# The seam between an attention stage and the dense tiles after it, reordered: the first tile's products inside the last attention pair, router logits in halves, butterflies in eight pieces

## What is computed

```python
x = x + tanh(g_xattn[0]) * ssm(ctx, layernorm(x));   x = x + tanh(g_ffn[0]) * quantised_ffn(layernorm(x))
x = x + tanh(g_xattn[1]) * attention16heads(layernorm(x), ctx)
x = x + tanh(g_ffn[1])   * moe(layernorm(x))          # 16 experts, top 4, + shared expert
x = x + tanh(g_xattn[2]) * map2(layernorm(x));        x = x + tanh(g_ffn[2]) * (fwht(silu(x@W1.T) * (x@W3.T)) @ W2.T)
x = x + tanh(g_xattn[3]) * map3(layernorm(x));        x = x + tanh(g_ffn[3]) * moe2(layernorm(x))   # 8 experts, top 2

# moe: logits = x @ gate_w.T; p = softmax(logits); the top k of p, renormalised, weigh the experts
#      h = silu(x @ w_gate.T) * (x @ w_up.T);  y += (h @ w_down.T) * weight[token, expert]
```

## Time and profile before

| | |
|---|---|
| three executions | 1054.9, 1059.25, 1060.66 us, median 1059.25 |
| the profiled execution | 1060.62 us, span 1058.4 us, mean granted clock 0.945 |
| busy | PE 940.8 (89%), DVE 729.5 (69%), ACT 646.8 (61%), POOL 485.2 (46%) |
| attention, a steady pair | 8.5 us |
| dense tiles | from 540.3 us to the end |
| clock slices | PE clock at 9 or 8 tenths only at the start, at the seam and at 565 to 595 us |

### The profile page before, as it was taken

One profiled execution on the slowest core, in us unless ns is written; L12 is line 12 of the kernel. 1 busy time (PEld: TensorE's weight loads), 2 busy tenths in 40 slices (PEclk: granted clock), 3 DMA queues, 4 the chain that ended last, 5 costly groups with the idle time before them and its releaser, 6 DMA issues.

```text
span 1058.4 us, 15635 instructions
## 1 busy us (share of the span) xinstructions
PE 940.8 (89%) x5402; PEld 768.4 (73%) x5402; DVE 729.5 (69%) x1309; ACT 646.8 (61%) x1251; POOL 485.2 (46%) x480
## 2 busy tenths in 40 slices
PE   5376677568999999999889999899999999999997
PEld 1033233346999999999878888787788888888886
DVE  6799998885777777776565765774565565666644
ACT  5857664665777777777535666545557545544553
POOL 0266551143666666765343334453343444444442
PEclk8599989687999999999889999999999999999999
DMA  9200100004000000000036000000000410000000
GB/s 314 113 0 1 60 1 0 1 1 176 2 2 1 2 1 1 2 1 2 1 134 264 1 1 1 1 2 1 1 1 1 166 58 2 1 2 1 20 1 21
DMA packets 4562, 35.92 MB, mean 34 GB/s; under 512 B 1021, under 2 KB 2149, under 8 KB 3109
## 3 DMA queue, kind: packets, MB, share of 16 engines
q1 hardware_dynamic: 4485, 34.93, 8.5%
HBM read 33.88 MB, written 1.05 MB: 33 GB/s over the span
## 4 chain that ended last, share of the span: by engine, by line
PE 47%; DVE 17%; issue 8%; POOL 8%; ACT 4%; DVEq 0%; POOLq 0%; ACTq 0%
PE psum L387 13%; PE psum L388 13%; PE psum L389 13%; POOL a_P L1890 3%; DVE a_max L1614 2%; POOL a_rk L1823 2%; POOL a_rq L1831 2%; DVE psum L1739 2%; DVE f_silu L1757 2%; PE psum L691 1%; PE psum L766 1%; PE psum L783 1%; PE psum L639 1%; ACT L1191 1%; PE psum L730 1%
## 5 line engine op out<-in xcount | busy, mean ns | idle before, releaser
L387 PE MATMUL psum<-x_norm_T_hi,f_wgu_hi 128*128 128x512 f32 x400 | 173.5, 434 | 3.8 <-DVE f_h_lo L1746 3.5
L388 PE MATMUL psum<-x_norm_T_lo,f_wgu_hi 128*128 128x512 f32 x400 | 158.9, 397 | 0.0
L389 PE MATMUL psum<-x_norm_T_hi,f_wgu_lo 128*128 128x512 f32 x400 | 158.4, 396 | 0.0
L826 ACT ACTIVATE f_h_hi<-psum 128x512 fp32r<-128x512 f32 x100 | 59.5, 595 | 107.7 <-DVE psum L1739 107.6
L387 PE MATMUL psum<-f_wd_hi,f_h_hi 128*128 128x256 f32 x400 | 121.5, 304 | 1.1 <-DVE f_h_lo L1746 0.9
L1746 DVE TENSOR_TENSOR f_h_lo<-psum,f_h_hi 128x512 fp32r<-128x512 f32 x100 | 69.0, 690 | 63.5 <-ACT f_h_hi L826 63.4
L388 PE MATMUL psum<-f_wd_lo,f_h_hi 128*128 128x256 f32 x400 | 112.7, 282 | 0.0
L389 PE MATMUL psum<-f_wd_hi,f_h_lo 128*128 128x256 f32 x400 | 112.6, 281 | 0.0
L1912 POOL TENSOR_TENSOR m_dBu<-m_du,m_Bs 128x1024 f32<-128x1024 f32 x32 | 76.1, 2381 | 69.2 <-DVE m_du L1333 24.8
L1836 POOL TENSOR_TENSOR f_wgu_lo<-f_w,f_wgu_hi 128x512 fp32r<-128x512 f32 x44 | 56.7, 1288 | 97.4 <-ACT f_wgu_hi L826 97.4
L1836 POOL TENSOR_TENSOR f_wgu_lo<-f_wb,f_wgu_hi 128x512 fp32r<-128x512 f32 x36 | 46.6, 1293 | 116.1 <-ACT f_wgu_hi L826 116.1
(11 more groups left out here) (329 smaller groups left out, 2716.6 us busy)
## 6 DMA issues: line engine op xcount, KB each, us to landing
f_wb<-in_f1b SPq DMA_DIRECT2D x1, 6912.0 KB, 20.1
f_w<-in_f3w SPq DMA_DIRECT2D x1, 5376.0 KB, 17.8
f_wa<-in_f1a SPq DMA_DIRECT2D x1, 3840.0 KB, 14.2
w_raw<-in_w0raw SPq DMA_DIRECT2D x1, 3072.0 KB, 18.5
f_w<-in_f2w SPq DMA_DIRECT2D x1, 3072.0 KB, 25.3
a_wo<-in_wo SPq DMA_DIRECT2D x2, 1024.0 KB, 13.1
a_wq<-in_wq SPq DMA_DIRECT2D x1, 2048.0 KB, 26.4
x_res<-in_x SPq DMA_DIRECT2D x1, 1024.0 KB, 8.9
```

The source lines that it names most:

```text
L387: mm(out, wh, xh, start=start, stop=False, **kw)
L388: mm(out, wh, xl, start=False, stop=False, **kw)
L389: return mm(out, wl, xh, start=False, stop=stop, **kw)
L826: return A(out_, in_, ACT.Copy)
```

## The change

The order of work changes; the number of matmuls and their shapes don't. DVE gets 12 more instructions.

- At the seam, `gate_up(0)` and the transposes of the combine weights go ahead of the last probability transposes (step 32), `combine(0)` and `gate_up(1)` ahead of the last output product (step 33). The last AC goes to bank 6, `combine(0)` to bank 7. ACT and POOL make the parts of tile 0 earlier, ACT loads the silu table in step 32.
- Router logits are two halves of 12 matmuls at two places.
- On DVE, `take_logits` moves behind the query sums, `router_top` ahead of `a_AC_lo` of step 31, `router_split` ahead of the last reciprocal, the residual of half 1 behind tile 1's `f_silu*up`.
- Beside the tiles, `aT` and `apply` of layer 2, half 0, leave the places of map steps; a normalise moves by one place; the four butterflies of two column blocks become eight of one, five of them at tiles 28 to 37.

```diff
+    AC_BANK = [4] * (HEADS2 - 1) + [6]
@@ the places
-    put_norm(1, 1, 3, 5, 6, 7, 9, 10, 13, 15, 18)
+    put_norm(1, 1, 3, 5, 6, 7, 8, 9, 10, 13, 15, 18)
-    put_attention(2, 0, P1 + 2, P1 + 4, P1 + 8, P1 + 12, P1 + 16, P1 + 20, P1 + 24)
+    put_attention(2, 0, P1 + 2, P1 + 4, P1 + 8, P1 + 13, P1 + 15, P1 + 18, P1 + 22)
-    for n, p in enumerate((44, 48, 52, P1)):
+    for n, p in enumerate((44, 48, 52, P1, P1 + 6, P1 + 10, P1 + 14, P1 + 19)):
         put(p, "butterfly", n)
-    put_norm(2, 0, P1 + 30, P1 + 32, P1 + 35, P1 + 37)
+    put_norm(2, 0, P1 + 30, P1 + 33, P1 + 35, P1 + 37)
@@ PE, attn1
                 if i == KB + 2:
-                    router_logits(1, 0).then_inc(S("b7_put"), 1)
+                    router_logits(1, 0, 0)
...
+                if i == HEADS2 - 2:
+                    router_logits(1, 0, 2).then_inc(S("b7_put"), 1)
                 if i + 1 < HEADS2:
                     query_sums(i + 1)
+                if i == HEADS2:
+                    pe.wait_ge(S("a_exp"), HEADS2)
+                    gate_up(0)
+                    pe.wait_ge(S("a_kT"), HEADS2)
+                    pe.wait_ge(S("f_cmb"), 1)
+                    combine_T(cmb_of(1, 0)).then_inc(S("b7_put"), 1)
...
-                if i == HEADS2:
-                    combine_T(cmb_of(1, 0)).then_inc(S("b7_put"), 1)
-                if i == HEADS2 + 1:
-                    gate_up(0)
...
+                if i == HEADS2 + 1:
+                    combine(0)
+                    gate_up(1)
@@ ACT, attn1
+                if i == HEADS2 - 1:
+                    gu_hi(0)
+                if i == HEADS2:
+                    A(scratch[:, 20:21], epsc[:, :], ACT.Silu)
+                    gu_hi(1)
+                    silu(0)
@@ DVE, attn1
+                if i == HEADS2 - 1:
+                    router_top(1, 0)
                 if i >= 2:
                     ac_lo(i - 2)
...
-                    router_top(1, 0)
+                    router_split(1, 0)
                 dve.wait_ge(S("a_exp"), i + 1)
...
-            router_split(1, 0)
...
+            silu_up(0)
@@ DVE, ffns
-                if g == 0:
+                if g == 1:
                     dve.wait_ge(S("a_out"), HEADS2)
                     residual("A1", 1)
@@ POOL
+                    if i == HEADS2 - 1:
+                        gu_lo(0)
```

More of the change, by code:

```diff
@@ L578, in gate_up, with combine, router_logits @@
                 last.then_inc(S("f_up" if b else "f_gate"), 1)
-        def router_logits(l, h):
+        def combine(g):
+            l, h, q, j = FT[g]
+            if not WEIGHTED[g]:
+                return
+            if j == (0 if l == 1 else J3S):
+                pe.wait_ge(S("b7_free"), bank7.index(("cmbT", l, h)) + 1)
+                loaded(pe, f"sel{l}")
+            if ROUTED[g]:
+                pe.wait_ge(S("f_h"), ROUTED[g])
+            mm(ps[:, 6 if g else 7, :], sel[l][:, j, :], cmbT[h][:, :], start=True, stop=True).then_inc(S("f_cw"), 1)
+        def router_logits(l, h, t0):
             xh, xl = xTp[h]
             pe.wait_ge(S("r_w"), 1 if l == 1 else 2)
-            for t in range(TH):
+            for t in (t0, t0 + 1):
                 sl = slice(t * P, (t + 1) * P)
@@ L732, in side @@
                     _, l, h = w
-                    use_bank7(w)
-                    last = router_logits(l, h)
+                    last = router_logits(l, h, 2)
+                elif kind == "logits_half":
+                    _, l, h = w
+                    use_bank7(("logits", l, h))
+                    router_logits(l, h, 0)
+                    continue
                 elif kind == "cmbT":
@@ L772, in ffns @@
         def ffns(k):
[L773 to L783, removed]
             def down(g):
@@ L1046, in d_hi, with silu @@
             copy(wdh[g % 3][:, :], raw_w(l, j)[:, GU:WJ]).then_inc(S("f_wdh"), 1)
+        def silu(g):
+            act.wait_ge(S("f_gate"), g + 1)
+            if g >= 2:
+                act.wait_ge(S("f_h" if WEIGHTED[g - 2] else "f_m"), ROUTED[g - 2] + 1 if WEIGHTED[g - 2] else g - 1)
+            A(sg[g % 2][:, :], ps[:, 2 + 2 * (g % 2), :], ACT.Silu).then_inc(S("f_sg"), 1)
         def router_exp(l, h):
@@ L1186, in ffns @@
                     rows_hi(g - 1)
-                if g < FN:
-                    act.wait_ge(S("f_gate"), g + 1)
-                    if g >= 2:
-                        act.wait_ge(S("f_h" if WEIGHTED[g - 2] else "f_m"), ROUTED[g - 2] + 1 if WEIGHTED[g - 2] else g - 1)
-                    A(sg[g % 2][:, :], ps[:, 2 + 2 * (g % 2), :], ACT.Silu).then_inc(S("f_sg"), 1)
+                if 0 < g < FN:
+                    silu(g)
                 side(2 * g)
@@ L1540, in router_split, with silu_up @@
             V.tensor_tensor(cmb[:, :, 64:64 + n], rr[:, :, 0:n], cmb[:, :, 32:32 + n], ALU.subtract).then_inc(S("f_cmb"), 1)
+        def silu_up(g):
+            dve.wait_ge(S("f_up"), g + 1)
+            dve.wait_ge(S("f_sg"), g + 1)
+            last = sg[g % 2][:, :] if WEIGHTED[g] else ps[:, 2 + 2 * (g % 2), :]
+            V.tensor_tensor(last, sg[g % 2][:, :], ps[:, 3 + 2 * (g % 2), :], ALU.mult).then_inc(S("f_m"), 1)
         def attn1(k, last_output):
@@ L1620, in attn1 @@
                     query_norms(i + 1)
+                    if i == HEADS2 - 2:
+                        dve.wait_ge(S("b7_put"), bank7.index(("logits", 1, 0)) + 1)
+                        take_logits(1, 0)
                     keys_lo(i + 1)
@@ L1752, in ffns @@
                     rows_lo(g - 1)
[L1753 to L1758 removed]
+                if 0 < g < FN:
+                    silu_up(g)
+                if g == 1:
                     dve.wait_ge(S("a_out"), HEADS2)
```

56 lines of the change are left out of this document (21 added, 35 removed).

## The result

The change takes 1047.98 us in the median, against 1059.95 of the kernel before in the same comparison; the ratio of their executions is 0.990 (95% interval 0.9869 to 0.9931), faster by more than the 0.5% that can be told. One of the six executions of the change took 1545.9 us at a mean granted clock of 0.552; it counts in the median (1047.24 without it) and not in the ratio. My forecast was 1046 in a range of 1040 to 1053.5. The profiled execution took 1051.76 us, 5.5 more than the 1046.3 of my sum, so the sum has faults that the median hides.

A forecast was written before the change was run, and what follows sets the result against it. PE was taken as the bound, losing time to waits and half clock at the seam and to waits at 560 to 800 us. Terms summed to -14.3 from the profiled 1060.6, 1046.3, rounded to 1046 us; range 1040 to 1053.5.

The forecast's parts named there:

- Seam -6.2: First logit to tile 2: starts 7.5 us earlier at full clock, less 1.3 for one half-clock stretch; bounds -3 and -8.3.
- the second wait: At the seam, PE stands 3.6 us for `a_AC_lo`, which comes only after `router_top`, slowed beside POOL.
- Residual and stats +0.9: Behind the seam, half 1's residual and stats follow each other on DVE, delaying `gate_up(3)` and the normalise: 0.9 us lost.
- The failed step: Next weights' loads start with the moved residual, some 6 us earlier, and are needed at tile 10; no loss charged.
- Logits in halves -1.7: The half-clock stretch at 566.6 goes if split narrow matmuls don't lower the clock: 1.7 us saved, bounds 0 and -1.7.
- Butterflies -2.8: Half-width pieces take 2.4 us, 0.95 less at each of the first three places: 2.8 us saved, bounds -1.5 and -4.3.
- Five more pieces +0.8: Butterfly pieces in tiles 28 to 37, beside residual, stats and normalise, cost 0.8 us; bounds 0 and +3.
- The stretch -1.7: The half-clock stretch at 679.2 should go with the butterfly waits: 1.7 us saved, bounds 0 and -1.7.
- Places of layer 2 -3.1 and -0.5: `aT` and `apply` off the map steps' places save 3.1 us of waits; the normalise behind `att_T` saves 0.5.
- that half clock moves with the waits: Rival, chance 0.30: half clock is moved, not removed; 1054.7 us with all five stretches back, 1050.5 with half.
- DVE isn't blocked: Rival, chance 0.13: POOL doesn't hold DVE up in `router_top`; 2.1 us more saved, 1044, with luck at the butterflies 1041.
- the clock falls only after idle: Rival, chance 0.08: half clock follows only idle stretches, so halving the logits gives nothing; 1048 us.

The follow-up runs named there:

- in the second: The changed kernel run again, unaltered, beside further kernels on one chip: median 1049.33 us, ratio 0.993 to the kernel before.
- top_late: The changed kernel with `router_top` moved back on DVE behind `a_PT_lo(30)`, so `a_AC_lo` goes first: ratio 0.9912 to the kernel before.
- maps_first: The changed kernel with the four small map weight loads issued ahead of the two large ones: ratio 0.9896 to the kernel before.
- logits_alone: The kernel before with only the three later router logits in halves: ratio 0.9986 to the kernel before.
- places_alone: The kernel before with only layer 2's transposes, applies and one normalise at the new places: ratio 0.9957 to the kernel before.
- butterflies_alone: The kernel before with only the butterflies in eight pieces at the change's places: ratio 1.0013 to the kernel before.
- rest_alone: The kernel before with the change's dense tiles (halved logits, eight butterflies, layer 2's places) but the old seam: ratio 0.9946 to the kernel before.

## Why the prediction was right, and where it wasn't

The median fell within the range and near the forecast, but that it came so near is luck. The sum has 14.3 us from the seam on, and between the two profiles 7.1 are there. Two errors of opposite sign hide it: I had not seen a loss of 4.8 us, and the sum was made against the profiled execution of before, which reached the seam later than all but three of the thirteen others. The medians differ by 12.0 us in the first comparison and by 7.5 in the second.

- **Seam -6.2**: measured 540.65 - 504.21 = 36.44 against 42.47 us, -6.0. The waits were 1.75, 3.23, none, 0.94 for my 1.8, 3.6, 1.0, 1.1. The half clock was mis-sized: 6.9 us long, 6.0 of it behind the wait, so it cost 3.0 and not 1.3, and it covered the third wait. That the second wait comes of `router_top` standing ahead of `a_AC_lo` is shown by `top_late`, and 2.14 us of it are the hold by GpSimd. Measured against the mean of five executions of the old seam the gain is 3.5 us with the residual's cost, since of the five only `before` has all three stretches of the earlier trace rows.
- **Residual and stats +0.9**: from tile 2 to tile 3's combine 12.41 against 11.23, +1.2. The 0.4 that I took off as the wait of before was already among the 8.7 of the seam's waits, so the sum takes it off twice; without that the term is +1.3.
- **The failed step** is the sentence "The loads of the next weights start with that residual, some 6 us earlier than before, and are needed at tile 10". They started 3.9 us earlier, not 6, while PE came to the map step 7.9 earlier, and the first map step at tile 6 waits for the last of the six loads, with 1.3 us to spare before. That was 4.7 us, shown by `maps_first`. I had looked for who waits for `f_wb` and not for what else hangs on the same queue.
- **Logits in halves -1.7**: -1.6, and `logits_alone` shows that the halving does it. The two of layer 3, which I put at nothing, give about as much again in the mean, 1.5 us at four of eight places.
- **Butterflies -2.8**: the three places wait 3.1 us instead of 4.3, so -1.2. A piece took 2.7 us, from 3.3, because the hold by POOL doesn't shrink with it (1.47 for the first instruction, from 1.73); and at the second and third place the 1.05 for `f_h_lo` stayed whole. **Five more pieces +0.8**: +0.7, two waits of 0.23 and 0.49. **The stretch -1.7**: gone in this profile, back in two later ones.
- **Places of layer 2 -3.1 and -0.5**: both exact, with 0.4 of new waits for `am_q`, and shown by `places_alone`. That two steps which share a bank, or a tile, add their delays I had counted as a risk of up to 0.8; in `butterflies_alone` it adds 1.7 us of waits, more than the pieces save.

The terms as measured: 1.64 + 6.0 - 1.2 + 1.6 - 4.8 + 1.2 - 0.7 + 1.7 + 3.6 - 0.4 = 8.6, against 8.8 between the profiles. Of the rivals, that half clock moves with the waits was partly true: one of the two stretches left is new. "DVE isn't blocked" and "the clock falls only after idle" are excluded, the latter by 8 of 12 whole logits, in which PE never stood, nor in the 5 us ahead of the four in layer 3. Why four of eight places in layer 3 and four of five at the seam kept full clock stays open. Of the signs that I named, the casts of `router_split` take 0.20 us, the clock is full behind all logits and two stretches are left; `w_mix` goes up to 1.47 us, just beyond my 1.4.

## What to carry to other kernels

When a change brings an engine forward, list every load that it will now meet, and on each queue what stands ahead of it: a small load behind large ones has their latency, and ahead of them it cost little here (0.6 us against the 4.7 won). Between two engines that hold each other up, put side work where the partner is idle, and behind whatever the bound engine waits for next. And hang side steps in gaps: splitting a step in two helped nothing that could be told, while moving it away from its neighbours gave 4.1 to 4.5 us.

## What the runs showed of the hardware

- An unchanged part of the kernel ahead of the seam took 499.15 to 507.34 us in fourteen profiles. One place of it is seen in the windows 220 to 240 and 240 to 260 us, first of before, then of `rest_alone`, 6.7 us ahead of it: the clock is 0.72 and 0.68 in the one and 0.83 and 0.91 in the other. The kernel before has the clock at half from 228.9 to 249.3 us, `rest_alone` only from 226.7 to 233.6 and from 247.2 to 250.6. So even one core's time carries some 8 us of chance, and parts of 2 to 5 us are told from stages, not from totals.

```profile
220.00:240.00 20.00, 12.42 (x64) 8.64 (x63) 16.41 (x34) 9.71 (x15) 9.98 (x7) 0.72 0.00 1
240.00:260.00 20.00, 18.12 (x88) 14.91 (x85) 10.95 (x27) 10.51 (x24) 7.23 (x9) 0.68 0.61 233
```

```profile
220.00:240.00 20.00, 11.70 (x71) 8.32 (x70) 16.06 (x33) 10.15 (x15) 9.99 (x7) 0.83 0.00 1
240.00:260.00 20.00, 15.97 (x95) 13.63 (x93) 14.56 (x33) 12.99 (x31) 11.07 (x15) 0.91 0.61 234
```

- Which DVE instructions POOL holds up. Beside the two of `router_top` above, in `top_late` even the 128x4 `a_neg_max` took 0.84 us (0.16 elsewhere) and ended with POOL's `f_wgu_lo`, while `a_max`, which reads PSUM, took its usual 1.23 beside POOL there, and `MATCH_REPLACE8` its usual 0.17 beside `a_P` in the changed kernel.
- Half clock behind PE waits: the 13 waits of 2.2 to 5.5 us at the seam and the map step all had a stretch with or behind them; of the fourteen waits of 1.75 us ahead of the AC of step 31, seven had one: three of five with the seam of before, four of nine with that of the change.
